# Small loads first, w_up's transpositions ahead of the first mixing, and gates ahead of weight spreading in the first steps of a two-layer kernel

## The chip, the cores and the metric

The kernel runs on one core of a Trainium2 chip. The metric is the device time of one execution in microseconds. The engines are named as in the profile: PE (TensorE), DVE (VectorE), ACT (ScalarE), POOL (GpSimd) and SP (SyncE, which here only issues DMAs). ACT and POOL issue DMAs too; SPq and ACTq are the queues' names.

## The reference

x is 128 batches of 32 channels by 512 columns. Two layers run one after the other, each with a mixing over channels, then a linear layer with a gated low-rank (LoRA) branch, then the residual sum:

```python
# layer 0
h = gelu(cond @ W0 + b0); h = gelu(h @ W1 + b1)          # 128 x 128 each
att = softmax(h @ W2 + b2)                                # 128 x 8, per batch
agg_w = einsum('bk,koi->boi', att, weight); agg_b = att @ bias_k
y = einsum('boi,bih->boh', agg_w, x) + agg_b[:, :, None]
top1 = argmax(y @ gate_w.T + expert_bias)                 # one of 4 experts
x1 = x + y @ W_up.T + (y @ lora_A[top1].T) @ lora_B[top1].T
# layer 1
c = conv1d(x1, weight, 9 taps, 4 groups) + (cond @ c_weight.T)[:, :, None] + fside
p = top2(softmax(c @ W_gate.T)), normalized               # of 8 experts
out = x1 + c @ W_base.T + b_base + sum(p * (c @ A.T) @ B.T)
```

## The kernel before

**Tiles and steps.** The 4096 rows of x are 32 tiles of 128 rows (4 batches). A software pipeline runs 34 steps; in step i TensorE does tile i's first layer (`up_half`, `turn_z`, `lora_delta`), tile i-1's convolution and base product (L1084, L1089), and the mixing `mix(i + 1)` for the next tile. All large products run as three passes over high and low parts of the operands (`up_hi`, `up_lo`, `y_hi`, `y_lo` and so on). Steps 0 to 3 are unrolled, and in steps 0 and 1 the rest of the preparation lies between the tiles' work.

**Order.** Every engine has one block of code and runs it in the order in which it is written; the engines meet in semaphores alone. What is queued behind a wait on an engine waits too.

**The way to the first tile.** The condition is turned (L887), copied (L650), and goes through the MLP: W0 (L890), W1 (L893) with a gelu behind each on ACT, then W2, a softmax, and `att_b`, the attention spread over lanes (L910, L685). The first MLP product waits for W0 and b0 together (`in_mlp[0]`). From `att_b` the mixing weights of a tile come in three steps: `make_prod` on POOL (L401, `prod`), `mix_sums` (L626, two sums `gsum`) and `mix_blocks` (L634, two halves of `mix_w`) on VectorE. Tiles 0 to 4 take their weights this way; from tile 5 they come out of `mix_all`, made at once by `mixb` (L1074, two products of `attT` and `wk_s`) and sent through DRAM. `mix(0, 0)` (L985) multiplies x's tile by these weights; `y_sum` (L644) adds the bias rows (`y`), `y_high` (ACT, L529) and POOL (L475) split it in parts.

**Fills.** All 13 weight operands are transposed by TensorE from the raw loads: `fill(n)` (L881), then `high_part(n)` on ACT (L505; L502 and L503 for `lora_b`), then `low_part(n)` on VectorE (L618, L615). The numbers: 0 to 3 are w_up's column blocks (`up_hi`, `up_lo`; four transpositions of 128x128 each), 4 the gate and `lora_a` rows, 5 (`LB_FILL`) `lora_b`, 6 to 9 `w_base`, 10 `a1` (the next layer's LoRA rows), 11 `bb1`, 12 the second gate. A fill waits for its bank to be free (`bank_free`): 6 for the low part 2, 7 for 3, 8 for 4, 9 for the context bias, 10 to 12 for 6 to 8. The upper halves of w_up's rows are loaded by SP, the lower by ACT (L483).

**Context and taps.** `wctx_s` is turned (L996), copied to `wctxT` (L695) and multiplied by the condition (L1003); `biasT` (L704) comes of it. The convolution's weights are shifted windows of the taps: ACT writes `taps_q` (L539), TensorE turns them in 16 pieces (L1014, into `ps_mix`), and `conv_hi` (L546) and `conv_lo` (L707) are their parts.

**A step.** `up_half(i, 1)` (L921, L926) makes the upper columns and the gate's logits; VectorE adds the bias (`gl`, L809), takes maximum and index, and masks z (`zm`, L825). In steps 0 and 1 `up_half(i, 0)` follows. `turn_z` (L960) transposes the mask, ACT and VectorE split it (`zT`, L516 and L735), `lora_delta` (L968) adds the low-rank product; then x1's two halves (L728), their way through the queues into `xq` (`move_x`, L294: SP five pieces, ACT three), and the next y. Between the instructions of the gate VectorE must wait for its own result, so `mix_sums` of tile i+2 stand there in the first steps (a `memset` of one column, `beat`, otherwise), and `mix_blocks` of tile i+1 ahead of the gate. In front of step 0's gate VectorE waits for `in_rows` (`ebias_s`, `bbase_s`), the last loads of SP's first list.

POOL does, in this order: the copies of `lora_b`, `make_prod(0)` and `(1)`, half of w_base's re-ordering, y_lo(0), the other half, `make_prod(2)`, `order_x(0, 0)` (L407, x's first tile in another order for the residual sum), then the small weights and `make_prod(3)`.

## Time and profile before

| | |
|---|---|
| median of 3 runs | 372.83 us (372.61 to 373.99) |
| the profiled execution | 373.17 us, of it 371.4 in the span |
| mean granted TensorE clock | 0.995 |
| busy share of the span | PE 94%, DVE 64%, POOL 54%, ACT 36% |
| moved by DMA | 31.98 MB, mean 86 GB/s |
| chain that ended last | PE 81%, DVE 4%, DMA 3%, issue 2%, ACT 1% |

The span begins with the first instruction and ends with the last. The profile page gives a mean over preparation and regular tiles; in its 40 slices of 9.3 us PE is at 2, 7, 9, 8 and 8 tenths in the first five, at 9 tenths (that is 90% or more) from the sixth on but for one 6 (the eighth slice, with the wait for `mix_all`), and at 7 and 5 in the last two. Times in the rows below are counted from the span's start.

### The profile page before, as it was taken

To read this page: it belongs to the slowest core of one execution; us is meant where nothing else is said; L and a number is where in the kernel's file an instruction comes from. 1 tells how busy PE (TensorE), PEld (TensorE's weight loads), DVE (VectorE), ACT (ScalarE), POOL (GpSimd) and SP (SyncE) were. 2 spreads that over 40 slices of the span, in tenths; PEclk is the share of its full clock that TensorE was granted. 3 is DMA by queue.
4 is the path that set the end of the run, shared out by engine and by line. 5 is a ranking of instruction groups with operands and counts; after the bars stand their busy time and mean duration, and the time that the engine had idled before them with its cause. 6 is when DMAs were issued, how large, how long until landed. Compare 5 with 4: busy or idle time off the path is not lost.

```text
span 371.4 us, 9133 instructions
## 1 busy us (share of the span) xinstructions
PE 349.1 (94%) x2593; PEld 341.9 (92%) x2593; DVE 238.1 (64%) x977; ACT 135.5 (36%) x410; POOL 199.7 (54%) x229
## 2 busy tenths in 40 slices
PE   2798899699999999999999999999999999999975
PEld 1686789699999999999999999999999999999974
DVE  1677768176666666666766666666667666666653
ACT  1645233134333443323333334333333333343330
POOL 8387546525456665555454565655455545566430
PEclk9999999899999999999999999999999999999999
DMA  7635268523333333333333333444333333332221
GB/s 151 193 103 132 52 170 172 107 46 70 80 77 76 80 85 85 85 85 72 70 57 79 77 76 81 85 85 85 85 64 73 60 80 77 75 83 57 60 58 58
DMA packets 54301, 31.98 MB, mean 86 GB/s; under 512 B 43868, under 2 KB 44300, under 8 KB 54288
## 3 DMA queue, kind: packets, MB, share of 16 engines
q1 hardware_dynamic: 40064, 27.69, 30.8%
q10 hardware_dynamic: 13984, 3.73, 7.2%
q0 software_dynamic: 240, 0.41, 0.4%
q8 instruction: 6, 0.10, 0.1%
q14 instruction: 7, 0.06, 0.0%
HBM read 14.35 MB, written 8.93 MB: 63 GB/s over the span
## 4 chain that ended last, share of the span: by engine, by line
PE 81%; DVE 4%; DMA 3%; issue 2%; ACT 1%; SPq 1%; ACTq 1%; DVEq 0%
PE ps_base L1084 18%; PE ps_up L921 17%; PE ps_base L1089 9%; PE ps_up L926 8%; PE ps_mix L985 7%; PE ps_mix L943 6%; PE ps_conv L943 6%; PE ps_base L1061 6%; PE ps_up L968 3%; DMA xq<-x1s 2%; PE ps_turn L952 1%; PE ps_turn L960 1%; DMA mix_all<-agg_mix 1%; SPq L294 1%; DVE mix_w L634 1%
## 5 line engine op out<-in xcount | busy, mean ns | idle before, releaser
L475 POOL TENSOR_TENSOR y_lo<-y,y_hi 128x512 fp32r<-128x512 f32 x31 | 40.0, 1291 | 123.8 <-ACT y_hi L529 123.8
L1084 PE MATMUL ps_base<-base_hi,c_hi 128*128 128x392 f32 (+1 forms) x256 | 78.2, 322 | 1.8 <-ACT c_hi L576 1.3
L1084 PE MATMUL ps_base<-base_lo,c_hi 128*128 128x392 f32 (+1 forms) x256 | 75.3, 311 | 0.0
L921 PE MATMUL ps_up<-up_hi,y_hi 128*128 128x292 f32 (+1 forms) x256 | 72.0, 304 | 3.1 <-DMA mix_all<-agg_mix 3.1
L921 PE MATMUL ps_up<-up_lo,y_hi 128*128 128x292 f32 (+1 forms) x256 | 69.7, 293 | 0.0
L454 POOL TENSOR_TENSOR xq_lo<-xq,xq_hi 128x260 fp32r<-128x260 f32 x64 | 47.5, 744 | 29.5 <-ACT xq_hi L511 29.5
L463 POOL TENSOR_TENSOR x1b<-x1s,bbase_s 128x256 f32<-128x256 f32 x64 | 56.5, 910 | 0.0
L921 PEld LDWEIGHTS ps_up<-up_hi,y_hi 128*128 128x128 f32 x256 | 49.0, 192 | 4.1 <-issue 4.1
L1084 PEld LDWEIGHTS ps_base<-base_hi,c_hi 128*128 128x128 f32 x256 | 48.2, 188 | 2.3 <-DVE ot L763 2.2
L921 PEld LDWEIGHTS ps_up<-up_lo,y_hi 128*128 128x128 f32 x256 | 49.0, 191 | 0.0
L1089 PE MATMUL ps_base<-base_hi,c_lo 128*128 128x392 f32 (+1 forms) x256 | 48.4, 311 | 0.0
L1084 PEld LDWEIGHTS ps_base<-base_lo,c_hi 128*128 128x128 f32 x256 | 48.1, 188 | 0.0
L511 ACT ACTIVATE xq_hi<-xq 128x260 fp32r<-128x260 f32 x64 | 27.0, 425 | 54.6 <-DMA xq<-x1s 54.6
L529 ACT ACTIVATE y_hi<-y 128x512 fp32r<-128x512 f32 x32 | 20.2, 632 | 69.9 <-DVE y L644 69.9
L926 PE MATMUL ps_up<-up_hi,y_lo 128*128 128x292 f32 (+1 forms) x256 | 43.2, 291 | 0.0
L1089 PEld LDWEIGHTS ps_base<-base_hi,c_lo 128*128 128x128 f32 x256 | 40.7, 189 | 0.0
L407 POOL COPY xtp<-xt 128x512 f32<-128x512 f32 x32 | 38.2, 1194 | 0.0
L926 PEld LDWEIGHTS ps_up<-up_hi,y_lo 128*128 128x128 f32 x256 | 36.9, 190 | 0.0
L576 ACT ACTIVATE c_hi<-ps_ct 128x256 fp32r<-128x256 f32 x64 | 21.1, 382 | 35.2 <-DVE ps_ct L755 35.2
L809 DVE TENSOR_TENSOR gl<-ps_up,ebias_s 128x4 f32<-128x4 f32 x32 | 5.2, 161 | 42.4 <-PE ps_up L926 42.4
L524 ACT ACTIVATE c<-ps_conv,biasT 128x64 f32<-128x64 f32 x128 | 29.7, 315 | 6.3 <-PE ps_conv L943 2.6
L755 DVE STREAM_TRANSPOSE ps_ct<-c 128x256 f32<-128x256 f32 x64 | 29.0, 455 | 1.0
(178 smaller groups left out, 655.0 us busy)
## 6 DMA issues: line engine op xcount, KB each, us to landing
xt<-in_x SPq DMA_DIRECT2D x32, 256.0 KB, 2.7
out_x<-ot SPq DMA_DIRECT2D x32, 256.0 KB, 2.0
xq<-x1s SPq DMA_DIRECT2D x160, 32.5 KB, 2.1
xq<-x1s ACTq DMA_DIRECT2D x96, 32.5 KB, 2.2
rows<-agg_rows SPq DMA_DIRECT2D x2, 597.0 KB, 5.0
wbase_raw<-in_L_ffn_W_base SPq DMA_DIRECT2D x2, 512.0 KB, 4.3
rows<-agg_rows SPq DMA_DIRECT2D x1, 598.0 KB, 4.7
wup_raw<-in_L_ffn_W_up ACTq DMA_DIRECT2D x2, 256.0 KB, 5.0
```

Of the source, the lines that this page charges most:

```text
L407: pool.tensor_copy(xtp[:, par].rearrange("p (j r m) -> p j r m", j=2, r=NQ), columns_of(xt[:, par]))\
L454: pool.tensor_tensor(xq_lo[:, gp], xq[:, gp], xq_hi[:, gp], ALU.subtract)\
L463: pool.tensor_tensor(columns_of(x1b[:, 1 - par])[:, j], shifted(j), columns_of(bbase_s[:])[:, j], ALU.add).then_inc(x1b_done, 1)
L475: pool.tensor_tensor(y_lo[:], y32[:], y_hi[:], ALU.subtract).then_inc(ylo_done, 1)
L511: act.activation(xq_hi[:, gp], xq[:, gp], ACT.Copy).then_inc(xqhi_done, 1)
L524: act.activation(c32[:, 0, cols], ps_of[0][:, 0, cols], ACT.Identity, bias=biasT[:, 0, bass.ds(t * SPT + b, 1)]).then_inc(c32_done, 1)
L755: dve.transpose(ps_ct[:, 0, gp * HALF:(gp + 1) * HALF], c32[:, gp]).then_inc(ct_done, 1)
L921: pe.matmul(into, y_hi[:, k], w[:, k, cols], start=(k == 0 and w is up_hi), stop=False, skip_group_check=True)
L926: mm = pe.matmul(into, y_lo[:, k], up_hi[:, k, cols], start=False, stop=(k == KC - 1), skip_group_check=True)
L943: mm = pe.matmul(ps_of[gp][:, 0, 0:HALF], w[:, gp, part], rhs[:, gp, :, part:part + NB], start=(n == 0 and part == 0), stop=(n == 2 and pa ...
L1084: pe.matmul(ps_base[:, j, 0:width], c_hi[:, q], w[:, q, j, 0:width], start=(q == 0 and w is base_hi), stop=False, skip_group_check=True)
L1089: mm = pe.matmul(ps_base[:, j, 0:width], c_lo[:, q], base_hi[:, q, j, 0:width], start=False, stop=(q == NQ - 1), skip_group_check=True)
```

## The change

Nothing is computed in another way; work changes its place.

- **Loads.** b0 and b1 leave SP's list and are the first two DMAs of ACT. The table load and its dummy activation follow, and ACT's two w_up loads come behind them. On SP `wmix_s` moves from ninth place to fourth.
- **Ahead of tile 0.** TensorE makes fills 0 to 3 in a row ahead of `mix(0, 0)`; the context's turn, its products and fills 4 and 5 stand behind it. ACT makes its high parts 0 to 5 and y_high(0) ahead of `taps_q`. VectorE makes low parts 0 to 2, y(0), low part 3, `wctxT`, low parts 4 and 5. POOL's `order_x(0, 0)` moves ahead of `make_prod(0)`.
- **Taps.** The 16 turns (now `turn_taps`) go from in front of tile 0's up-projection to the end of step 0, behind fill 12; `conv_hi` and `conv_lo` go with them, and TensorE's wait for `conv_lo` from the mixing of tile 1 to the convolution of step 1.
- **Step 0.** `turn_z` no longer waits behind fills 6 to 8: fills 6 and 7 stand between it and `lora_delta(0)`, and 8 to 12 behind `mix(1)`. ACT makes y_high(1) and its three moves right behind high parts 6 and 7; high parts 8 to 12 come behind them.
- **Gates 0 and 1.** VectorE's `mix_blocks(1)` and `(2)` go behind the mask `zm` of steps 0 and 1, and `mix_sums(2)` and `(3)` from between the gate's instructions to behind the next tile's y; `beat` memsets take their places.

The diff, cut to its core:

```diff
--- before.py
+++ after.py
@@ -308,13 +308,11 @@
             sp.dma_start(cond_s[:], cond).then_inc(in_cond, 16)
             sp.dma_start(W0_s[:], W0).then_inc(in_mlp[0], 16)
-            sp.dma_start(b0_s[:], b0.rearrange("(p a) -> p a", a=1)).then_inc(in_mlp[0], 16)
             sp.dma_start(W1_s[:], W1).then_inc(in_mlp[1], 16)
-            sp.dma_start(b1_s[:], b1.rearrange("(p a) -> p a", a=1)).then_inc(in_mlp[1], 16)
+            sp.dma_start(wmix_s[:], wmix.rearrange("k o i a -> o k (i a)")).then_inc(in_mix, 16)
             sp.dma_start(W2_s[:], W2).then_inc(in_mlp[2], 16)
             sp.dma_start(b2_s[:], b2.partition_broadcast(P)).then_inc(in_mlp[2], 16)
             sp.dma_start(biask_s[:], bias_k).then_inc(in_bias, 16)
-            sp.dma_start(wmix_s[:], wmix.rearrange("k o i a -> o k (i a)")).then_inc(in_mix, 16)
@@ -411,6 +409,8 @@
             cp.then_inc(lb_copied, 1)
+            pool.wait_ge(x_in[0], 16)
+            order_x(0, 0)
             pool.wait_ge(attb_ready, 1)
             pool.wait_ge(wmix_ready, 1)
             make_prod(0)
@@ -436,8 +436,6 @@
             make_prod(2)
-            pool.wait_ge(x_in[0], 16)
-            order_x(0, 0)
@@ -478,12 +476,14 @@
+            act.dma_start(b0_s[:], b0.rearrange("(p a) -> p a", a=1)).then_inc(in_mlp[0], 16)
+            act.dma_start(b1_s[:], b1.rearrange("(p a) -> p a", a=1)).then_inc(in_mlp[1], 16)
+            act.wait_ge(ident_ready, 1)
+            act.activation(h1T[:, 0:1], ident[:, 0:1], ACT.Gelu).then_inc(table_loaded, 1)
             for half in range(2):
                 q2 = slice(half * NQ // 2, (half + 1) * NQ // 2)
                 act.dma_start(wup_raw[NB:P, q2], w_up.rearrange("(m j q) h -> j m q h", j=2, q=NQ)[1, :, q2])\
                     .then_inc(in_up[half], 16)
-            act.wait_ge(ident_ready, 1)
-            act.activation(h1T[:, 0:1], ident[:, 0:1], ACT.Gelu).then_inc(table_loaded, 1)
             act.wait_ge(in_mlp[0], 32)
@@ -531,6 +531,10 @@
             act.activation(ex[:], lg[:], ACT.Exp, bias=negm[:, 0:1], accum_out=exsum[:, 0:1]).then_inc(exp_done, 1)
+            for n in range(LB_FILL):
+                high_part(n)
+            y_high(0)
+            high_part(LB_FILL)
@@ -538,12 +542,6 @@
-            for n in range(LB_FILL):
-                high_part(n)
-            y_high(0)
-            high_part(LB_FILL)
-            act.wait_ge(conv_turned, 1)
-            act.activation(conv_columns(conv_hi), conv_turns(), ACT.Copy).then_inc(convhi_ready, 1)
@@ -558,16 +556,13 @@
-                if isinstance(i, int) and i == 0:
-                    high_part(NF1)
-                    high_part(NF1 + 1)
                 if once(i - 1):
                     conv_out(i - 1)
                 if once(i):
                     z_high(i)
                 if isinstance(i, int) and i == 0:
-                    for n in range(NF1 + 2, NF2):
-                        high_part(n)
+                    high_part(NF1)
+                    high_part(NF1 + 1)
                     y_high(1)
@@ -583,8 +578,10 @@
                 if isinstance(i, int) and i == 0:
-                    for n in range(NF2, NF):
+                    for n in range(NF1 + 2, NF):
                         high_part(n)
+                    act.wait_ge(conv_turned, 1)
+                    act.activation(conv_columns(conv_hi), conv_turns(), ACT.Copy).then_inc(convhi_ready, 1)
@@ -688,24 +685,20 @@
-            low_part(0)
-            low_part(1)
-
+            for n in range(NQ - 1):
+                low_part(n)
+            dve.wait_ge(rows_in[0], 16)
+            y_sum(0)
+            low_part(NQ - 1)
             dve.wait_ge(wctx_turned, 1)
             dve.tensor_copy(wctxT[:], ps_conv[:, 0, 0:C].rearrange("p (g o) -> p g o", g=GP).unsqueeze(2)
                             .to_broadcast([P, GP, NP, CG])).then_inc(wctx_copied, 1)
-            low_part(2)
-            dve.wait_ge(rows_in[0], 16)
-            y_sum(0)
-            for n in range(3, NF1):
-                low_part(n)
+            low_part(NQ)
+            low_part(LB_FILL)
             dve.wait_ge(ctx_done, 1)
...
-            dve.wait_ge(convhi_ready, 1)
-            dve.tensor_tensor(conv_columns(conv_lo), conv_turns(), conv_columns(conv_hi), ALU.subtract)\
-                .then_inc(conv_ready, 1)
             mix_sums(1, 0)
@@ -800,22 +793,19 @@
-                elif soon(i + 1):
-                    mix_blocks(i + 1, 0)
-                    mix_blocks(i + 1, 1)
                 if once(i):
...
                     dve.wait_ge(gate0_step, i * G0 + 1)
-                    if soon(i + 2):
+                    if soon(i + 2) and once(i - 2):
                         mix_sums(i + 2, 0)
...
-                    if soon(i + 2):
+                    if soon(i + 2) and once(i - 2):
                         mix_sums(i + 2, 1)
@@ -828,8 +818,9 @@
-                if isinstance(i, int) and i == 0:
-                    low_part(NF1)
+                if isinstance(i, int) and i < 2:
+                    mix_blocks(i + 1, 0)
+                    mix_blocks(i + 1, 1)
@@ -838,7 +829,7 @@
                 if isinstance(i, int) and i == 0:
-                    low_part(NF1 + 1)
+                    low_part(NF1)
@@ -853,9 +844,15 @@
                 if once(i + 1):
                     y_sum(i + 1)
+                if isinstance(i, int) and i < 2:
+                    mix_sums(i + 2, 0)
+                    mix_sums(i + 2, 1)
                 if isinstance(i, int) and i == 0:
-                    for n in range(NF1 + 2, NF):
+                    for n in range(NF1 + 1, NF):
                         low_part(n)
+                    dve.wait_ge(convhi_ready, 1)
+                    dve.tensor_tensor(conv_columns(conv_lo), conv_turns(), conv_columns(conv_hi), ALU.subtract)\
+                        .then_inc(conv_ready, 1)
                     dve.wait_ge(mixb_done, 2)
@@ -977,8 +974,6 @@
-                if isinstance(t, int) and t == 1:
-                    pe.wait_ge(conv_ready, 1)
@@ -989,32 +984,33 @@
-            fill(0)
-            fill(1)
+            for n in range(NQ):
+                fill(n)
+            pe.wait_ge(aggb_ready, 1)
+            mix(0, 0)
             pe.wait_ge(in_ctx, 16)
             pe.wait_ge(attb_ready, 1)
             pe.transpose(ps_conv[:, 0, 0:C], wctx_s[:], ident[0:C, 0:C]).then_inc(wctx_turned, 1)
-            fill(2)
-            pe.wait_ge(aggb_ready, 1)
-            mix(0, 0)
-
+            fill(NQ)
             pe.wait_ge(wctx_copied, 1)
             for gp in range(GP):
                 mm = pe.matmul(ps_conv[:, 0, gp * B:(gp + 1) * B], wctxT[:, gp].rearrange("c p o -> c (p o)"), condT[:],
                                start=True, stop=True)
             mm.then_inc(ctx_done, 1)
-            for n in range(3, NF1):
-                fill(n)
-
-            pe.wait_ge(taps_ready, 1 + GP)
-            pe.wait_ge(y32_done, 1)
-            for part in range(2):
-                for p in range(NP):
-                    s = part * NP + p
-                    mm = pe.transpose(ps_mix[:, 0, s * C:(s + 1) * C],
-                                      taps_q[:, part * NP + NP - 1 - p].rearrange("o g i q -> o (g i q)"),
-                                      ident[0:C, 0:C])
-            mm.then_inc(conv_turned, 1)
+            fill(LB_FILL)
+
+            def turn_taps():
+
...
+                pe.wait_ge(taps_ready, 1 + GP)
+                pe.wait_ge(y32_done, 2)
+                for part in range(2):
...
+                mm.then_inc(conv_turned, 1)
@@ -1027,10 +1023,9 @@
                 if isinstance(i, int) and i == 0:
-                    for n in range(NF1, NF2 - 1):
-                        fill(n)
                     pe.wait_ge(fill_lo, NF1)
                 if isinstance(i, int) and i == 1:
+                    pe.wait_ge(conv_ready, 1)
                     pe.wait_ge(consts_ready, 3)
@@ -1049,7 +1044,8 @@
                     if isinstance(i, int) and i == 0:
-                        fill(NF2 - 1)
+                        fill(NF1)
+                        fill(NF1 + 1)
                     lora_delta(i)
@@ -1065,8 +1061,9 @@
-                    for n in range(NF2, NF):
+                    for n in range(NF1 + 2, NF):
                         fill(n)
+                    turn_taps()
...
```

On TensorE, from w_up's transpositions to tile 0's first up-projection (L921, after L918). Names: `wup_raw` is w_up, `ga_raw` fill 4, `lb_rep` fill 5; 128x128 and the like are the output's shape. Before:

```order
L881 MATMUL ps_up<-ident,wup_raw 128x128 x8
L996 MATMUL ps_conv<-ident,wctx_s 128x32
L881 MATMUL ps_base<-ident,wup_raw 128x128 x4
L985 MATMUL ps_mix<-mix_w,xt 128x128 x4
L1003 MATMUL ps_conv<-condT,wctxT 128x128 x2
L881 MATMUL ps_base<-ident,wup_raw 128x128 x4
L881 MATMUL ps_ct<-ident,ga_raw 128x36 x4
L881 MATMUL ps_turn<-ident,lb_rep 96x128 x4
L1014 MATMUL ps_mix<-ident,taps_q 128x32 x16
L921 MATMUL ps_up<-up_hi,y_hi 128x292
```

After:

```order
L878 MATMUL ps_up<-ident,wup_raw 128x128 x8
L878 MATMUL ps_base<-ident,wup_raw 128x128 x8
L980 MATMUL ps_mix<-mix_w,xt 128x128 x4
L993 MATMUL ps_conv<-ident,wctx_s 128x32
L878 MATMUL ps_ct<-ident,ga_raw 128x36 x4
L997 MATMUL ps_conv<-condT,wctxT 128x128 x2
L878 MATMUL ps_turn<-ident,lb_rep 96x128 x4
L918 MATMUL ps_up<-up_hi,y_hi 128x292
```

All of w_up's sixteen transpositions now stand ahead of the mixing, the context behind it, and the taps are gone from this stretch.

On VectorE, around gate 0, from the context's bias `biasT` to the low part of z (`zT`). Before:

```order
L704 TENSOR_TENSOR biasT<-ps_conv,fside_s 128x256
L707 TENSOR_TENSOR conv_lo<-ps_mix,conv_hi 128x16x2x16
L626 TENSOR_REDUCE gsum<-prod 128x16 x2
L634 TENSOR_TENSOR mix_w<-gsum,quad 128x64 x2
L809 TENSOR_TENSOR gl<-ps_up,ebias_s 128x4
L626 TENSOR_REDUCE gsum<-prod 128x16
L816 MAX m<-gl 128x8
L626 TENSOR_REDUCE gsum<-prod 128x16
L822 MAX_INDEX ix<-m,gl 128x8
L825 SCALAR_TENSOR_TENSOR zm<-iota_e,ix,ps_up 128x96
L618 TENSOR_TENSOR base_lo<-ps_base,base_hi 128x2x256
L735 TENSOR_TENSOR zT<-ps_turn,zT 32x128
```

After:

```order
L700 TENSOR_TENSOR biasT<-ps_conv,fside_s 128x256
L623 TENSOR_REDUCE gsum<-prod 128x16 x2
L799 TENSOR_TENSOR gl<-ps_up,ebias_s 128x4
L805 MEMSET beat 128x1
L806 MAX m<-gl 128x8
L811 MEMSET beat 128x1
L812 MAX_INDEX ix<-m,gl 128x8
L815 SCALAR_TENSOR_TENSOR zm<-iota_e,ix,ps_up 128x96
L631 TENSOR_TENSOR mix_w<-gsum,quad 128x64 x2
L728 TENSOR_TENSOR zT<-ps_turn,zT 32x128
```

The taps' low part and the two halves of tile 1's weights leave the place ahead of the gate; the weights now stand between the mask and z's low part.

On ScalarE, from z's high part in step 0 to the last plane of the preparation (`base_hi` and `b_hi` are the high parts of fills 6 to 12). Before:

```order
L546 ACTIVATE conv_hi<-ps_mix 128x16x2x16
L505 ACTIVATE base_hi<-ps_base 128x2x256 x2
L516 ACTIVATE zT<-ps_turn 96x128
L505 ACTIVATE base_hi<-ps_ct 128x2x256
L505 ACTIVATE base_hi<-ps_conv 128x2x256
L529 ACTIVATE y_hi<-y 128x512
L294 DMA xq<-x1s 128x1x65 x3
L505 ACTIVATE base_hi<-ps_base 128x4x128
L505 ACTIVATE b_hi<-ps_base 128x4x128
L505 ACTIVATE base_hi<-ps_ct 128x4x8
L589 ACTIVATE mix_b<-ps_conv 128x16x32
```

After:

```order
L543 ACTIVATE taps_q<-taps,parity_of 32x16x64 x2
L516 ACTIVATE zT<-ps_turn 96x128
L505 ACTIVATE base_hi<-ps_base 128x2x256 x2
L529 ACTIVATE y_hi<-y 128x512
L294 DMA xq<-x1s 128x1x65 x3
L505 ACTIVATE base_hi<-ps_ct 128x2x256
L505 ACTIVATE base_hi<-ps_conv 128x2x256
L505 ACTIVATE base_hi<-ps_base 128x4x128
L505 ACTIVATE b_hi<-ps_base 128x4x128
L505 ACTIVATE base_hi<-ps_ct 128x4x8
L584 ACTIVATE conv_hi<-ps_mix 128x16x2x16
L586 ACTIVATE mix_b<-ps_conv 128x16x32
```

Two planes of w_base (from `ps_ct` and `ps_conv`) have moved from ahead of tile 1's y_hi to behind the three moves, and `conv_hi` to the end.

## Rows read from the trace of the kernel before

**Rows 1.** The stretches (start:end, length, busy us of PE, PEld, DVE, ACT, POOL, clock, DMA, GB/s).
```profile
2.50:7.10 4.60, 0.45 (x1) 0.18 (x1) 0.55 (x4) 0.98 (x2) 4.60 (x8) 1.00 0.94 177
...
70.57:74.00 3.43, 3.43 (x14) 3.43 (x15) 0.13 (x1) 0.00 (x0) 1.19 (x2) 0.51 0.10 35
...
90.70:360.00 269.30, 268.35 (x2047) 267.87 (x2046) 176.32 (x764) 99.11 (x318) 146.04 (x158) 1.00 0.35 76
```

**Rows 2.** Timeline: start, duration, engine, line, work, count, idle time before and its releaser.
```profile
0.75 1.21 ACTq L483 DMA_DIRECT2D wup_raw<-in_L_ffn_W_up  x2
...
3.26 0.29 DVE L650 COPY condT<-ps_mix 128x128 f32<-128x128 f32 x1 [0.50 <-PE ps_mix L887]
...
7.11 0.80 PE L890 MATMUL ps_mix<-condT,W_s 128*128 128x128 f32 x2 [3.89 <-DMA b_s<-in_L_cond_b]
```

**Rows 3.** The DMA issues: count, KB each, us from issue to landing.
```profile
cond_s<-in_cond SPq DMA_DIRECT2D x1, 64.0 KB, 1.9
...
b_s<-in_L_cond_b SPq DMA_DIRECT2D x2, 0.5 KB, 5.4
```

**Rows 4.** Timeline of TensorE, 14 to 23 us.
```profile
14.64 1.92 PE L881 MATMUL ps_up<-ident,wup_raw 128*128 128x128 f32 x8
...
17.71 1.89 PE L985 MATMUL ps_mix<-mix_w,xt 128*128 128x128 f32 x8
...
19.44 0.61 PE L1003 MATMUL ps_conv<-condT,wctxT 128*128 128x128 f32 x4
...
21.35 1.17 PE L1014 MATMUL ps_mix<-ident,taps_q 32*128 32x32 f32 x16
...
22.46 0.40 PE L921 MATMUL ps_up<-up_hi,y_hi 128*128 128x292 f32 x1
```

**Rows 5.** Timeline of VectorE, 25 to 31 us.
```profile
25.15 1.40 DVE L634 TENSOR_TENSOR mix_w<-gsum,quad 128x64 f32<-128x64 f32 x2
...
26.47 0.15 DVE L809 TENSOR_TENSOR gl<-ps_up,ebias_s 128x4 f32<-128x4 f32 x1
...
27.55 0.31 DVE L825 SCALAR_TENSOR_TENSOR zm<-iota_e,ix,ps_up 128x96 f32<-128x96 f32 x1
...
28.63 0.28 DVE L735 TENSOR_TENSOR zT<-ps_turn,zT 32x128 fp32r<-32x128 f32 x1 [0.17 <-ACT zT L516]
...
30.41 0.69 DVE L644 TENSOR_TENSOR y<-ps_mix,rows 128x512 f32<-128x512 f32 x1
```

**Rows 6.** Timeline of TensorE, ScalarE and ScalarE's DMA queue, 31 to 41 us.
```profile
31.14 2.06 ACTq L294 DMA_DIRECT2D xq<-x1s  x3
...
32.44 1.09 PE L1074 MATMUL ps_conv<-wk_s,attT 8*128 8x512 f32 x2 [0.22 <-DVE base_lo L618]
...
33.24 0.60 ACT L505 ACTIVATE base_hi<-ps_base 128x512 fp32r<-128x512 f32 x1 [1.48 <-issue]
...
34.32 0.40 PE L921 MATMUL ps_up<-up_hi,y_hi 128*128 128x292 f32 x1
...
39.89 0.31 PE L960 MATMUL ps_turn<-ident,zm 128*96 128x128 f32 x1 [0.80 <-DVE zm L825]
...
40.90 0.50 PE L968 MATMUL ps_up<-lb_w,zT 96*128 96x256 f32 x2 [0.70 <-DVE zT L735]
```

**Rows 7.** Timeline of GpSimd, first product; then xt's loads issued before 40 us.
```profile
15.40 0.72 POOL L401 TENSOR_TENSOR prod<-wmix_t,att_b 128x256 f32<-128x256 f32 x1 [5.78 <-DVE att_b L685]
...
DMA to landing us min/median/max: 2.5/4.3/4.6
```

**Rows 8.** The line of mix_w (count, min/median/max ns, us); its longest half in the timeline.
```profile
L634 DVE TENSOR_TENSOR mix_w<-gsum,quad x10: 224/714/1344, 16.7 to 57.4; 128x64 f32<-128x64 f32 x10
...
55.90 1.29 POOL L475 TENSOR_TENSOR y_lo<-y,y_hi 128x512 fp32r<-128x512 f32 x1 [3.63 <-ACT y_hi L529]
...
55.93 1.34 DVE L634 TENSOR_TENSOR mix_w<-gsum,quad 128x64 f32<-128x64 f32 x1 [1.03 <-PE ps_base L1089]
```

**Rows 9.** Timeline of TensorE behind its wait for `mix_all`.
```profile
70.57 0.58 PE L921 MATMUL ps_up<-up_hi,y_hi 128*128 128x292 f32 x1 [3.13 <-DMA mix_all<-agg_mix]
```

5 lines of the change are left out of this document (added).

## The prediction

> **What bounds the kernel now.** I read the stretches first. From 90.70 to 360.00 TensorE is busy 268.35 of 269.30 us [rows 1]: the regular tiles leave nothing to win, and no edit touches them. What can change is how early they are reached, so the sum is made over the way to tile 1's LoRA product (`lora_delta(1)`, at 40.90), behind which both kernels run nearly the same instructions. Next the loads: the first matmul of the conditioning MLP starts at 7.11, after 3.89 us of waiting for a bias [rows 2] whose load takes 5.4 us, while cond_s, issued ahead of it, takes 1.9 [rows 3]; the DMA engines are 94% busy from 2.50 to 7.10 [rows 1]. Then, in order of time, TensorE up to its first up-projection [rows 4], VectorE between there and y(1), the mixed input of tile 1 [rows 5], and the way from y(1) to lora(1) [rows 6].
>
> **A. The small loads.** b0 and b1 go to ACT's queue and are issued first; ACT's two w_up loads (1.21 us of issuing [rows 2]) go behind the table load and its dummy activation. The transposed condition is copied by 3.55 (3.26 + 0.29 [rows 2]), so the first matmul could start at 3.6 where it starts at 7.11, if b0 and W0 have landed. Price of b0: between 1.9, as for cond_s (0.75 + 1.9 = 2.65, hidden under 3.6), and 5.4 as now (0.75 + 5.4 = 6.15). I take the low end: what was ahead of the biases in the engines were ACT's 512 KB, and these are now issued after them. ACT's two issues end near 4.5 (from 3.3, where the dummy activation starts now, plus 1.21), just when the first gelu wants ACT (3.6 + 0.80 + 0.1). wmix, moved from ninth to fourth on SP, is wanted some two us later than it lands. So the chain up to the spread attention comes **3.5 us earlier**. It cannot gain more, since the condition's own load and copy are not moved.
>
> **B. Fills ahead of the first mixing.** TensorE reaches w_up's fills at 11.1 in place of 14.64 [rows 4] and now makes all sixteen transpositions in a row. Eight took 1.92, so sixteen take 3.84 and end at 15.0. The mixing weights are ready at 14.2 (the mixing started at 17.71, less 3.5), so the mixing starts at 15.0, 2.7 earlier; 0.8 of A is lost here. Its eight passes took 1.89, at the slow rate of the transpositions (0.24 us each; the four passes at 19.44 take 0.15 each [rows 4]). The dense block may bring the fast rate sooner: between 0.95 and 1.89, I take 1.5. Its end then lies 3.1 earlier, at 16.5. From there y(0), 0.69 [rows 5], a low plane of equal width, 0.69, the copy of wctxT, 0.4, the context products, 0.6, and lora_b's four transpositions, 0.5 at the fast rate, give 19.4 for the first up-projection, which started at 22.46 [rows 4]: **3.1 earlier**. The sixteen transpositions of the taps (1.17 [rows 4]) no longer stand ahead of it; they come back in D.
> On POOL the copy of x's first tile (`order_x(0, 0)`) now stands ahead of the first product, and the mixing weights behind that. The product started at 15.40 [rows 7] and is wanted at 11.9; a POOL pass this wide takes up to 1.29 [rows 8], so the copy is covered if the tile lands by 10.6. SP issued it at 6.20 and now does so about 1.0 earlier, with two issues fewer ahead; such loads took 4.3 in the median and 4.6 at most [rows 7]: 9.5 to 9.8. Covered, by one us.
>
> **C. Gate 0 ahead of the mixing weights.** Before gate 0 (`gl`, 26.47) VectorE made conv_lo (as wide as y, 0.69) and tile 1's weights `mix_w` (1.40 [rows 5]); both leave, 2.1. Against that, lora_b's planes begin only with the fill that now stands right ahead of the up-projection, where 1.17 of taps lay between; between 0.5 and 1.17 comes back, I take 0.8, because ACT's y_hi(0) is now ahead of these planes instead of among them. So gl is 3.1 + 2.1 - 0.8 = 4.4 earlier. The gate, 1.39 from gl to the end of the mask `zm` (27.86), loses two sums and gets two memsets: between 0.8 and 1.39, I take 1.1, so zm comes 4.7 earlier. Now mix_w(1) sits between zm and z's low part, where 0.77 of waiting and one plane stood (27.86 to 28.63 [rows 5]); at 1.40 that is 0.6 back. **z's low part, and 2.5 behind it as now the end of y(1) (31.10), come 4.1 earlier**, y(1) at 27.0.
> mix_w's price is the uncertain one here. Its ten halves took 0.224 to 1.344, 0.714 in the median [rows 8], so two lie between 0.45 and 2.7. The longest starts 0.03 us after a POOL subtraction of 1.29 and ends 0.08 behind it [rows 8]. I keep 1.40, since POOL copies rows there then as now.
> The Trainium skill ("SBUF — State Buffer", section "SBUF: two separate sides") says that a VectorE instruction with two SBUF inputs and a GpSimd one that reads SBUF lock each other out: the later one waits for the whole earlier one. The row of that longest half agrees. By that rule a half would cost 0.22 when POOL is idle, and the edit would win 0.95 more than I count.
> A wait moves too: gl(0) is now the first behind `in_rows`, the last loads of SP's list. They come about 3.4 earlier by the order of issue; I cost it at nothing, and if they are late by more than the one us of slack, gl and all behind it wait for them.
>
> **D. Taps and spare planes behind tile 1's mixing.** So far ACT made base's third and fourth high planes before y(1). Now they stand behind y_hi(1) and ACT's three xq moves, which end 2.10 after y(1) (31.14 + 2.06 - 31.10 [rows 6]). Then come one high plane, 0.60 [rows 6], its low plane, 0.69, and TensorE's gate fill, 0.5 (y(1) to 32.44 is 1.34 now, less the low plane and 0.15 of waiting for the next one); then the taps, 1.17; then the two mix products, 1.88 (32.44 to 34.32 [rows 6]). So tile 1's up-projection starts 2.10 + 0.60 + 0.69 + 0.50 + 1.17 + 1.88 = 6.9 behind y(1), where it starts 3.2 behind it: **3.7 given back**, and 0.4 of the 4.1 is left. The cover is gone because ACT, not TensorE, now sets this stretch; queued behind its moves are five planes, conv_hi and mix_b.
>
> **E. Gate 1.** mix_w(2) leaves the place ahead of gate 1. TensorE's wait at z's transposition (0.80, for zm) goes, since zm is now ready under the convolution; the wait at lora(1) (0.70, for z's low part [rows 6]) stays about as long, with conv's sum and one transposition ahead of it on VectorE. **0.85 won**, between 0.5 and 1.5 (both waits). For tile 2 the weight sums move behind y(2), POOL's next product waits for them, and y_lo(2) is queued behind that; TensorE waits for tile 1's xq moves right behind y_lo(2)'s use, so I cost it at nothing; without that cover it is some tenths.
>
> **Sum.** 4.1 - 3.7 + 0.85 = 1.25, say 1.3 us. On the profiled execution (373.17, of it 371.4 span) that is 371.9; the median of the runs, 372.83, lies 0.34 below it: **371.5**. Ends: A between 1.0 and 3.5, B half a us either way, mix_w between 0.95 better and 1.3 worse, D between 3.2 and 4.2.
>
> **Rivals.** *The dense block pays more.* Sixteen transpositions without a gap bring TensorE to the fast rate before the mixing (0.95, 0.5 better than my 1.5), and mix_w(1) meets POOL between two copies (0.5 better). For it: both rates and both lengths occur in this trace; against it: POOL's copies stand in the same order. 371.5 - 1.0 = 370.5.
> *The biases land no earlier* (the end on the other side). Place: the first W0 matmul, which waits for b0. Its load is 0.5 KB and took 5.4 us [rows 3]; if that is its own time and not the queue's, the chain starts at 6.15, 2.55 later than my 3.6: 374.0. It decides at 3.6 + 1.3 = 4.9: a landing beyond that makes the kernel slower than before. Against it: the biases stood behind the w_up loads, at engines 94% busy.
> *Clock.* D leaves TensorE little to do for some 4 us before tile 1's up-projection, with one gap near 1.8. Behind the gap of 3.13 in front of 70.57 [rows 9] the granted clock is 0.51 until 74.00, that is the level of 1.2 GHz [rows 1]. If this comes up here, half the clock over 3.43 us loses 1.7: 373.2. Against it: that gap is nearly twice as long. The Trainium skill ("TensorE: Matmul & The Clock Gate", section "HAM oscillation — how this bites in real kernels") warns of idle gaps that re-throttle TensorE; the gap of 3.13 agrees, and no row here shows what a shorter one does.
> *x late.* The upper half of w_up is issued over 2 us later and shares the engines with x's first tile. If that lands at 12.3, not by 10.6, POOL's first product is held 1.7: 373.2. Against it: the latest such load took 4.6, not 7.
>
> **How the numbers follow.** Forecast 0.55, dense block 0.22, biases 0.07, clock 0.08, x late 0.08. The likeliest gives 371.5, by itself 370.8 to 372.4. The range 370.2 to 373.4 takes in all but the biases' 374.0 and the tails. A measurement of this kernel can tell about 0.5% from no change, 1.86 us: below 370.97 lie nearly all of the dense block and the forecast's low edge, 0.26; above 374.69 only late biases with something added, 0.03; between them 0.71.
>
> **What would show it.** Right: the first W0 matmul near 3.6, the mixing near 15, y(1) ending near 27, tile 1's up-projection still near 34 and behind ACT's moves, lora(1) near 39.6. Wrong: a W0 matmul beyond 4.9; a product on POOL that waits for x; a granted clock near half between 28 and 38; a tile 1 up-projection well before 33, which would mean that ACT's moves don't hold the planes.

## The result and the profile after

The change made the kernel slower: 378.17 us in the median against 372.72 of before (four executions of each). The ratio on record is 1.0114 with a 95% interval of 1.0064 to 1.0163; that of these two medians is 1.0146. Forecast were 371.5 and a range of 370.2 to 373.4, so both the time and the sign were missed. The profiled execution took 378.09 us, of it 376.2 in the span: 4.8 over the 371.4 of before.

The page of the changed kernel (the busy tenths and the granted clock in 40 slices, here of 9.4 us) already shows where. Before, the only slice under full clock near the start was the eighth, behind the wait for `mix_all`. Now the fourth and fifth slices, 28 to 47 us, are at 8 and 7 tenths too:

```profile
span 376.2 us, 9139 instructions
...
PE   2877899699999999999999999999999999999985
...
PEclk9998799989999999999999999999999999999999
```

The way through it on TensorE, from the timeline (start, duration, engine, line, work, idle time before and its releaser):

```profile
3.99 0.77 PE L887 MATMUL ps_mix<-condT,W_s 128*128 128x128 f32 x2 [0.47 <-DVE condT L647]
...
9.47 0.60 PE L893 MATMUL ps_mix<-W_s,h2T 128*128 128x8 f32 x2 [3.34 <-DMA b_s<-in_L_cond_b]
...
17.47 1.46 PE L980 MATMUL ps_mix<-mix_w,xt 128*128 128x128 f32 x8
...
21.61 0.38 PE L918 MATMUL ps_up<-up_hi,y_hi 128*128 128x292 f32 x1
...
32.90 0.38 PE L878 MATMUL ps_ct<-ident,g_p 8*128 8x8 f32 x4 [1.91 <-DVE base_lo L615]
...
35.07 1.61 PE L1071 MATMUL ps_turn<-wk_s,attT 8*128 8x512 f32 x2
36.61 0.61 PE L918 MATMUL ps_up<-up_hi,y_hi 128*128 128x292 f32 x1
...
42.24 0.40 PE L940 MATMUL ps_conv<-xq_hi,conv_hi 128*128 128x256 f32 x2
...
45.04 0.50 PE L965 MATMUL ps_up<-lb_w,zT 96*128 96x256 f32 x2 [1.09 <-DVE zT L728]
...
75.23 0.37 PE L918 MATMUL ps_up<-up_hi,y_hi 128*128 128x292 f32 x1 [3.73 <-DMA mix_all<-agg_mix]
```

Against [rows 2, 4, 5, 6, 9] and the sum on record, in us:

| | before | forecast | after |
|---|---|---|---|
| first MLP product | 7.11 | 3.6 | 3.99 |
| first mixing starts | 17.71 | 15.0 | 17.47 |
| tile 0's up-projection | 22.46 | 19.4 | 21.61 |
| mask zm(0) ready | 27.86 | 23.2 | 25.57 |
| y(1) ends | 31.10 | 27.0 | 29.23 |
| tile 1's up-projection | 34.32 | 33.9 | 36.61 |
| tile 1's LoRA product | 40.90 | 39.6 | 45.04 |
| end of the wait for mix_all | 70.57 | | 75.23 |

Two things stand out. The first product came 3.1 earlier, near the forecast's 3.5, but the first mixing only 0.24: the gain was gone within 6 us, in a wait for another bias. And between y(1) and lora(1) 6 us were lost, part of them at half clock. The stretches of the changed kernel (columns as in [rows 1]):

```profile
30.00:35.00 5.00, 2.73 (x26) 2.14 (x27) 3.08 (x5) 3.19 (x6) 2.70 (x3) 1.00 0.73 176
36.00:42.00 6.00, 6.00 (x24) 5.39 (x24) 2.31 (x11) 0.82 (x3) 3.08 (x4) 0.50 0.00 0
```

and the same two of the kernel before:

```profile
30.00:35.00 5.00, 4.18 (x25) 2.67 (x24) 3.03 (x6) 2.39 (x5) 3.42 (x4) 1.00 0.48 68
36.00:42.00 6.00, 4.50 (x36) 4.10 (x35) 5.72 (x18) 2.19 (x9) 4.93 (x6) 1.00 0.27 92
```

From 30 to 35 TensorE had 2.73 us of work in place of 4.18; from 36 to 42 it was busy throughout, with 24 records in place of 36, at 0.50, the level of 1.2 GHz.

One thing is needed to read the runs below. The mean granted clock differs from one execution of a kernel to the next, and the time follows it: before took 371.4 to 373.3 at 0.994 or 0.995, and 375.4 to 376.8 at 0.979 to 0.983. So each kernel is given by its mean clock too, as median us (number of executions). Three executions that are on record as slow (377.07 and 377.94 of before, 375.98 of the mended loads in the old order) count in the first column alone. The columns are coarse, some hold one or two executions, and differences within one are rough:

| kernel | median | 0.993 and over | 0.988 to 0.991 | 0.985 to 0.986 | up to 0.983 |
|---|---|---|---|---|---|
| before, three sets measured beside the runs | 373.3 | 372.3 (31) | 373.8 (20) | 374.3 (6) | 375.9 (7) |
| changed | 378.2 | | | 377.4 (2) | 378.6 (2) |
| changed, last gap filled | 376.6 | | 375.3 (4) | 375.8 (1) | 377.9 (5) |
| changed, planes first | 374.6 | 373.3 (1) | 373.9 (2) | 374.6 (4) | 377.0 (3) |
| changed, loads mended | 377.5 | | | | 377.5 (10) |
| changed, both mended | 373.7 | | | 373.1 (6) | 375.1 (6) |
| changed, all gaps filled | 380.7 | | 376.7 (1) | | 381.9 (3) |
| before, loads alone | 373.5 | 371.6 (2) | 373.2 (5) | 376.4 (1) | 376.5 (2) |
| before, loads mended | 372.5 | 369.6 (2) | 372.0 (4) | 373.4 (2) | 372.7 (3) |
| before, planes late | 376.8 | | 375.9 (3) | 377.5 (2) | |
| before, mix_all early | 368.3 | 368.2 (4) | 369.7 (2) | | |
| before, loads mended, mix_all early | 366.0 | 365.6 (4) | 369.3 (2) | | |

### The profile page after: what moved, and what is told of

Its sections match the earlier page's. It is cut to its first block, busy times and chain, and to the rows that moved or that the text cites. A ratio compares the mean times of both kernels' runs of the same rounds, so it can differ in the third digit from the quotient of the medians.

```text
span 376.2 us, 9139 instructions
## 1 busy us (share of the span) xinstructions
PE 351.5 (93%) x2593; PEld 344.5 (92%) x2593; DVE 240.2 (64%) x981; ACT 135.9 (36%) x410; POOL 200.2 (53%) x229
## 4 chain that ended last, share of the span: by engine, by line
PE 86%; DMA 4%; DVE 4%; issue 2%; SPq 2%; ACT 1%; ACTq 1%; DVEq 0%
PE ps_base L1081 18%; PE ps_up L918 17%; PE ps_base L1086 9%; PE ps_up L923 9%; PE ps_mix L980 7%; PE ps_mix L940 6%; PE ps_conv L940 6%; PE ps_base L1057 6%; PE ps_up L965 3%; DMA xq<-x1s 2%; DMA b_s<-in_L_cond_b 2%; PE ps_turn L949 1%; DMA mix_all<-agg_mix 1%; PE ps_turn L957 1%; SPq L294 1%
## 5 line engine op out<-in xcount | busy, mean ns | idle before, releaser
L918 PE MATMUL ps_up<-up_hi,y_hi 128*128 128x292 f32 (+1 forms) x256 | 72.5, 306 | 3.7 <-DMA mix_all<-agg_mix 3.7
L918 PE MATMUL ps_up<-up_lo,y_hi 128*128 128x292 f32 (+1 forms) x256 | 70.3, 295 | 0.0
L918 PEld LDWEIGHTS ps_up<-up_hi,y_hi 128*128 128x128 f32 x256 | 49.6, 194 | 5.3 <-issue 5.3
L918 PEld LDWEIGHTS ps_up<-up_lo,y_hi 128*128 128x128 f32 x256 | 49.7, 194 | 0.0
L529 ACT ACTIVATE y_hi<-y 128x512 fp32r<-128x512 f32 x32 | 20.2, 632 | 70.9 <-DVE y L641 67.4
L923 PE MATMUL ps_up<-up_hi,y_lo 128*128 128x292 f32 (+1 forms) x256 | 44.3, 296 | 0.1
```

The lines of the kernel that those rows point to most:

```text
L918: pe.matmul(into, y_hi[:, k], w[:, k, cols], start=(k == 0 and w is up_hi), stop=False, skip_group_check=True)
L923: mm = pe.matmul(into, y_lo[:, k], up_hi[:, k, cols], start=False, stop=(k == KC - 1), skip_group_check=True)
```

## Experiments on the loads

**The loads alone, in the kernel before.** The edit is the SP, ACT and `wmix_s` part of the diff, nothing else.

> The kernel before, with the order of the loads alone (part A). Theory: the first product starts near 4.0 in place of 7.11, but the W2 product still near 9.5 (for b2), so the first mixing starts 0.3 to 0.6 before 17.71, and as nothing else is moved, the time is 0.2 to 0.7 less than before: 372.0 to 372.5, the clock as before. Rival, the sum on record for part A: the mixing 2.5 to 3.5 earlier and the time with it: 369.3 to 370.3. Second rival: the loads disturb each other (w_up and x land later): 373 or more.

W2's product waited for b2 until 9.06, the first mixing started at 16.72 and lora(1) at 39.77, 1.13 earlier:

```profile
16.72 1.67 PE L985 MATMUL ps_mix<-mix_w,xt 128*128 128x128 f32 x8
...
39.77 0.50 PE L968 MATMUL ps_up<-lb_w,zT 96*128 96x256 f32 x2 [0.70 <-DVE zT L735]
```

On the way to tile 1 the theory holds, with a little more won than expected (1.0 at the mixing, 0.3 to 0.6 expected), and the 3.5 on record for part A are refuted without any other part of the change. In the time it isn't shown. The median is 373.47 against 373.69 (ratio 1.0009, 0.9961 to 1.0058) where 372.0 to 372.5 were expected. At equal clock the differences go both ways: 0.7 and 0.6 faster in the upper two columns (seven executions), 2.1 and 0.6 slower in the lower two (three). One more thing is in this profile: in spite of the 1.13 won the wait for `mix_all` ended at 70.60, where it ended at 70.57 before [rows 9]:

```profile
70.60 0.58 PE L921 MATMUL ps_up<-up_hi,y_hi 128*128 128x292 f32 x1 [4.62 <-DMA mix_all<-agg_mix]
```

**b2 and GpSimd's zeros, in the changed kernel.** VectorE's copy of wmix had gone from 0.68 us to 2.69. These are the rows of the changed kernel, then that of before:

```profile
5.40 3.54 POOL L394 MEMSET mix_all<- 128x4096 f32 x1
...
6.78 2.69 DVE L649 COPY wmix_rep<-wmix_s 32x1024 f32<-32x1024 f32 x1 [2.94 <-DMA wmix_s<-in_L_cond_weight]
```

```profile
9.55 0.68 DVE L652 COPY wmix_rep<-wmix_s 32x1024 f32<-32x1024 f32 x1 [6.00 <-DMA wmix_s<-in_L_cond_weight]
```

The zeros lie at 5.40 to 8.94 in both kernels. Before, wmix landed behind them; loaded earlier, it starts its copy inside them, and the copy ends 0.53 behind their end, at 9.47: as if it had started at 8.8. The softmax's logits stand behind it on VectorE. So two covers lay over each other, b2 (W2 at 9.47) and the zeros (VectorE till 9.6). Three runs take them away singly and together (cuts of the edits, with a remark behind two lines):

```diff
-            sp.dma_start(b2_s[:], b2.partition_broadcast(P)).then_inc(in_mlp[2], 16)
+            act.dma_start(b2_s[:], b2.partition_broadcast(P)).then_inc(in_mlp[2], 16)   # behind b1
...
-            pool.memset(mix_all[:], 0.0).then_inc(mix_zero, 1)
+                if isinstance(i, int) and i == 1:                                       # in the step
+                    pool.memset(mix_all[:], 0.0).then_inc(mix_zero, 1)
```

b2 alone:

> The changed kernel with b2 on ScalarE's queue behind b0 and b1; GpSimd's zeros stay at 5.40. Theory, two covers: the W2 product starts at 6.8 to 7.7 in place of 9.47, but the copy of wmix still takes about 2.7 and ends about 0.5 behind the zeros, near 9.5, and the logits lg come behind it and lane_rep, at 9.6 to 9.8 in place of 10.18; the first mixing 0.3 to 0.6 earlier than 17.47. Rival, b2 alone held the chain: lg near 8.4, the mixing near 15.7.

The zeros alone:

> The changed kernel with GpSimd's zeros for mix_all in step 1; b2 stays sixth on SP's queue. Theory, two covers: the copy of wmix takes 0.7 to 0.8 in place of 2.69, but the W2 product still waits for b2 until 8.6 to 9.5, and lg comes 0.7 behind it; the first mixing within 0.8 of 17.47. Rival, the engines were held by the zeros in another way too (b2's landing): W2 before 8.4 and the mixing before 16.

Both:

> The changed kernel, with b2's load third on ScalarE's queue in place of sixth on SP's, and GpSimd's 3.54 us of zeros for mix_all moved from 5.40 into step 1 (behind x1b). Theory, two covers for one another: the W2 product waits for b2 until 9.47, and the copy of wmix (2.69 us in place of 0.68, ending 0.53 behind GpSimd's zeros) would hold VectorE till 9.61 in any case; without both the W2 product starts at 7.7 (when W2 lands), the logits lg near 8.4 in place of 10.18, the first mixing near 15.7 in place of 17.47, y(1) ends near 27.4 in place of 29.23. The gap and the half clock behind it stay, so the time is 1.5 to 2 less than the changed kernel: 376.2 to 376.7. Rival: the loads of w_up and x, which now land 7.0 to 7.2 after their issue, or the copy of x ahead of the first product (11.81 to 13.05), hold the mixing: at most 0.7 less, 377.5 or more.

Singly, the logits came at 9.63 and 9.70 in place of 10.18: half a microsecond from either, as the two covers say. With b2 alone W2's product started at 7.03 while the copy took 4.13 (5.35 to 9.48); with the zeros alone the copy took 0.68 while W2's product waited for b2 until 8.99:

```profile
6.52 0.68 DVE L650 COPY wmix_rep<-wmix_s 32x1024 f32<-32x1024 f32 x1 [2.64 <-DMA wmix_s<-in_L_cond_weight]
...
8.99 0.60 PE L894 MATMUL ps_mix<-W_s,h2T 128*128 128x8 f32 x2 [2.83 <-DMA b_s<-in_L_cond_b]
```

Together: W2 at 6.79, lg at 7.50, the first mixing at 14.58 (forecast of the record: 15.0):

```profile
14.58 1.13 PE L981 MATMUL ps_mix<-mix_w,xt 128*128 128x128 f32 x8
```

Each of the single runs was executed once, and neither was faster than the changed kernel: 379.70 at 0.982 with b2 alone, 379.04 at 0.979 with the zeros alone. Even the half microsecond was lost again in the single runs, where the mixing started at 17.35 and 17.47. The rows of the run with b2 alone show to whom:

```profile
5.35 4.13 DVE L649 COPY wmix_rep<-wmix_s 32x1024 f32<-32x1024 f32 x1 [1.44 <-DMA wmix_s<-in_L_cond_weight]
...
10.82 1.02 DVE L663 TENSOR_SCALAR att<-ex,exrec 128x8 f32<-128x8 f32 x1
```

```profile
10.71 1.09 POOL L404 COPY xtp<-xt 128x512 f32<-128x512 f32 x1 [0.62 <-DMA xt<-in_x]
```

`order_x(0, 0)`, which the change put ahead of the first product, ran from 10.71 to 11.80, and VectorE's `att`, 0.23 us in the profile of the changed kernel, ended at 11.84. In the run with the zeros alone `att_spread` took 1.33 in place of 0.42 under the same copy.

With both taken away, too, the time didn't follow the mixing: 377.46 in the median (376.2 to 376.7 were expected), all ten executions at 0.974 to 0.982. y(1) ended at 27.35, 1.9 earlier than without the mending, but the clock now fell near 30.9, and the taps, the two mix products and the up-projection ran at half clock: tile 1's up-projection started at 36.82 (36.61 without). The time is about the rival's (377.5 or more), the mechanism isn't: the mixing did come.

**The mended loads in the old order.** The same edits on the kernel before:

> The kernel before, with the order of the loads (part A), b2 on ScalarE's queue behind b0 and b1, and GpSimd's zeros for mix_all moved into step 1. Part A as the sum on record meant it, in the old order. Theory: as with the same loads in the changed order (lg 7.50, first mixing 14.58), the first mixing starts 2.7 to 3.1 before the 17.71 of before, tile 1's LoRA product near 38.2 in place of 40.90, and the time at equal granted clock is 2 to 2.7 less: 369.6 to 370.3 where the mean clock is 0.995 (before: 371.4 to 373.2, 15 of 31 executions). Rival 1, mix_all: with the loads alone lora(1) came 1.13 earlier and the wait for mix_all still ended at 70.60 (70.57 before); if its landing doesn't follow, the time at 0.995 is 371.5 to 372.3. Rival 2, the clock: a shorter way means the same work with TensorE idle at other places; fewer than a third of the executions keep 0.995 and the median is no better than before.

At 0.995 the two executions took 369.56 and 369.70, 2.6 less than before at that clock: the theory, and what part A is worth when nothing else holds the chain (0.9 to 3.2 less in the other columns). The median, 372.47, is 0.85 less (ratio 0.997, 0.9938 to 1.0002, so not clear of no change). Two of the twelve executions kept 0.995, where eight of the 24 of before beside them had 0.994 or 0.995: rival 2 holds in part. Rival 1 fell. The profiled execution is one at 0.985, so no profile shows the way of those two; in it the first mixing started at 14.62, the clock fell twice, and lora(1) came at 42.62.

## Experiments on the planes behind the moves

**Planes first.** High parts 8 and 9 go back ahead of y_high(1) and the three moves, in the changed kernel:

```diff
-                    high_part(NF1)
-                    high_part(NF1 + 1)
+                    for n in range(NF1, NF2):
+                        high_part(n)
                     y_high(1)
...
-                    for n in range(NF1 + 2, NF):
+                    for n in range(NF2, NF):
                         high_part(n)
```

> The changed kernel, with high parts 8 and 9 back ahead of tile 1's y_hi and ScalarE's three moves, as before the change; all else as changed. Theory, the planes behind the moves (part D): fills 10 to 12 and the taps no longer wait for the end of the moves (31.38); the taps start near 31.1 in place of 33.14, tile 1's up-projection near 34.0 in place of 36.61, no gap of TensorE is over 1 us there, the clock stays at 1.00, and lora(1) comes near 40.0 in place of 45.04: 5 us less, 373 us. Rival, the clock has another cause (the order of the step, the lower load of the engine over a longer stretch): the up-projection is 2 to 2.6 earlier but at half clock, lora(1) near 42.5: 375.5 to 376.2. Second rival: tile 1's moves, issued 0.7 later by ScalarE, hold the convolution: lora(1) over 41, 374 or more.

In the changed kernel the first of the two planes starts when ScalarE's moves have been issued. These are its rows, then the taps of this run:

```profile
29.27 2.11 ACTq L294 DMA_DIRECT2D xq<-x1s  x3
...
31.43 0.60 ACT L505 ACTIVATE base_hi<-ps_ct 128x512 fp32r<-128x512 f32 x1 [1.53 <-PE ps_base L878]
```

```profile
32.36 1.15 PE L1009 MATMUL ps_mix<-ident,taps_q 32*128 32x32 f32 x16
```

The median fell from 378.17 to 374.56, and at equal clock by 2.8 (0.985 to 0.986) and 1.6 (up to 0.983). In the profiled execution the taps started 1.97 behind y(1)'s end (30.39 to 32.36) in place of 3.91 (29.23 to 33.14). The time lies between the theory's 373 and the first rival's 375.5: the order was undone as expected, but the clock still fell in all but one execution to under 0.993.

**Planes late, in the kernel before.** The opposite: the two planes go behind the moves, everything else stays.

> The kernel before, with high parts 8 and 9 behind tile 1's y_hi and ScalarE's three moves: part D's ScalarE side alone; the taps stay where they were. Theory (the price on record for D less the taps): the two mix products wait for low part 9, the moves end 2.10 after y(1), then come two high planes and a low one; tile 1's up-projection starts near 36.9 in place of 34.32, 2.6 later, TensorE has a gap of 2 us or more in front of it, and the time at equal clock is 1.8 to 2.6 over before; with lower clocks in most executions the median is 376 to 377.5. Rival: the stretch behind the up-projection (waits of 0.80 and 0.70 before) takes the delay up: less than 1 over before at equal clock, and 0.995 as often as before.

At equal clock it took 2.1 and 3.2 more than before, the median 376.78 against 373.32 (ratio 1.0096, 1.0062 to 1.0130): over half of the whole loss, from the order of two planes and the clock that fell behind it. TensorE's fill of the gate (fill 12) in the kernel before, then rows of this run, ScalarE's queue and ScalarE first, then TensorE:

```profile
31.84 0.38 PE L881 MATMUL ps_ct<-ident,g_p 8*128 8x8 f32 x4 [0.60 <-DVE base_lo L618]
```

```profile
30.74 2.06 ACTq L294 DMA_DIRECT2D xq<-x1s  x3
...
32.84 0.60 ACT L505 ACTIVATE base_hi<-ps_ct 128x512 fp32r<-128x512 f32 x1 [1.48 <-issue]
...
34.31 0.56 PE L879 MATMUL ps_ct<-ident,g_p 8*128 8x8 f32 x4 [3.46 <-DVE base_lo L616]
...
36.74 1.91 PE L1072 MATMUL ps_turn<-wk_s,attT 8*128 8x512 f32 x2
...
38.58 0.61 PE L919 MATMUL ps_up<-up_hi,y_hi 128*128 128x292 f32 x1
```

The planes start when the moves have been issued (32.80), TensorE waits 3.46 for the low part, and at 34.3 the clock has fallen: the second mix product takes 1.91 in place of 1.02 at full clock. The up-projection starts 4.26 later than [rows 6]. Of that 2.47 stand at the gate's fill already (34.31 against 31.84), where 2.6 were expected for the order; the other 1.79 are added behind it, at half clock.

**Both mended.** The changed kernel with the mended loads and the planes first:

> The changed kernel with both parts mended: b2 and GpSimd's zeros as in the other run, and high parts 8 and 9 ahead of tile 1's y_hi and ScalarE's moves. Theory: y(1) ends near 28 (27.35 with the loads mended, plus up to 0.7), tile 1's up-projection starts 4.9 behind it at full clock, near 32.9, lora(1) near 38.9; at 0.995 that is 370 to 370.8, at 0.982 to 0.986 (three or four stretches at half clock) 373 to 375. Rival: with TensorE busy 7.4 to 7.5 of 10 us in 10 to 20 and 20 to 30 (8.7 and 9.1 before), the clock falls early in nearly every execution, as in the run with the loads mended alone (0.974 to 0.982 in all ten), and the median stays over 374.5.

373.68 in the median, ratio 1.002 (0.9994 to 1.0045). At 0.985 to 0.986 it takes 373.1 where before takes 374.3 and the mended loads in the old order 373.4; up to 0.983 it takes 375.1 against their 375.9 and 372.7 (but three of its six had 0.977, lower than any of the other). So the changed order, mended, is no worse than before at equal clock; whether it is as good as the old order with the same loads stays open. None of its twelve executions kept 0.988 or more, where 21 of the 24 of before beside them did. That is the rival's mechanism; its median, over 374.5, didn't come. In its profile the clock fell first near 20.2, after TensorE had been busy 3.14 of 5 us from 15 to 20.

## Experiments on the clock

**The gap in front of fill 12 filled.** Sixteen transpositions of the identity stand in it; the taps overwrite their result.

```diff
+                    pe.wait_ge(y32_done, 2)
+                    for s in range(16):
+                        pe.transpose(ps_mix[:, 0, 0:P], ident[:], ident[:])
                     fill(NF - 1)
```

> The changed kernel, with sixteen transpositions of the identity (their result is overwritten by the taps) between fill 11 and fill 12, where TensorE now waits 1.91 us (30.99 to 32.90). Theory, the clock: the granted clock falls to 0.50 from 35.3 to 42.6 because of that gap; filled, it stays at 1.00, mix_b's second product takes 1.1 in place of 1.61 and tile 1's up-projection (36.61 to the convolution at 42.24, 5.63) about 3.2, as before the change (34.32 to 37.46); lora(1) then comes near 42.2 in place of 45.04 and the time is 2.5 to 3 less than the changed kernel's 378.2: 375.2 to 375.7. Rival, the order alone: lora(1) is late because of what stands ahead of tile 1's up-projection, the clock falls for another reason or the wait behind it takes the gain: 377.7 to 378.5.

376.64: half the expected gain. Five of ten executions had 0.986 or 0.991, the others 0.982. In the profile TensorE was busy 4.84 of the 5 us from 30 to 35, and the clock still fell, at 36.3 and for 3.4 us in place of 6.8 (35.4 to 42.2): tile 1's up-projection took 4.67 (35.59 to 40.26) in place of 5.63. So the gap of 1.91 is not the only cause; that it made things worse rests on the times and on one profile of each kernel.

**All gaps filled.** Six, five and four more transpositions ahead of the context products, `turn_z` of tile 0 and fill 11:

> The changed kernel with 31 transpositions of the identity in TensorE's waits between 19.5 and 33 us (six ahead of the context products, five ahead of turn_z of tile 0, four ahead of fill 11, sixteen ahead of fill 12); their results are overwritten. Theory, the clock follows how busy TensorE was in the stretch before: with only the last gap filled, five of ten executions had a mean clock of 0.991 in place of 0.982 to 0.986; with all four filled, most have 0.991 or more, and the median is near 375 (at 0.991 the run with one gap filled took 374.3 to 376.3). Rival: what TensorE does ahead of 19 us or the random place of the fall decides; the clock stays at 0.982 to 0.986 in half of the executions or more, median 376 to 377.5.

The median, 380.74, is worse than the rival's: three of the four executions ran at 0.973 to 0.982. As a way to a faster kernel this fell. But the profiled execution, the one at 0.991, had full clock from the start to 70 us, and so shows what the changed order does without the clock. Its timeline on TensorE:

```profile
33.02 0.38 PE L878 MATMUL ps_ct<-ident,g_p 8*128 8x8 f32 x4 [0.25 <-DVE base_lo L615]
...
35.19 1.02 PE L1084 MATMUL ps_turn<-wk_s,attT 8*128 8x512 f32 x2
36.13 0.40 PE L918 MATMUL ps_up<-up_hi,y_hi 128*128 128x292 f32 x1
...
39.29 0.40 PE L940 MATMUL ps_conv<-xq_hi,conv_hi 128*128 128x256 f32 x2
...
42.09 0.51 PE L965 MATMUL ps_up<-lb_w,zT 96*128 96x256 f32 x2 [1.09 <-DVE zT L728]
```

The mixing (17.52) and the end of y(1) (29.26) are those of the changed kernel within 0.05. The up-projection starts 6.87 behind y(1) (6.9 on record for part D), takes 3.16 in place of 5.63, and lora(1) comes at 42.09: 1.19 later than before by the order, and 2.95 earlier than in the changed kernel, which is the clock's part in one profile of each. Why this execution still took 376.74: of the 3.5 by which its span is over that of before, 1.2 stand at the end of the wait for `mix_all` (71.80) and 2.3 behind it, and most of these are seen at the other end, in a stretch at half clock while the last tiles run out (length, PE busy, clock, DMA share, GB/s):

```profile
362.00:366.00 4.00, 3.31 (x17) 0.57 0.01 2
```

## Experiments on the wait for mix_all

**All four loads of mix_all in step 2, in the kernel before.**

```diff
-                if isinstance(i, int) and i in (2, 3):
+                if isinstance(i, int) and i == 2:
...
-                    for s in range((i - 2) * SPT // 2, (i - 1) * SPT // 2):
+                    for s in range(SPT):
```

> The kernel before, with all four loads of mix_all issued in step 2 (before: two in step 2, two in step 3); nothing else is changed. In eight of the ten profiles so far the span was the end of TensorE's wait for mix_all plus 300.7 to 301.1, so whatever moves ahead of it counts only as far as that load moves too. Theory: issued near 56.8 to 59.3 the last load lands by 64.5, ahead of 67.4, when TensorE began to wait for it; the wait of 3.13 goes and with it the stretch at half clock behind it (3.43 us at 0.51, 1.7): 4 to 5 less than before, 367.5 to 369. Rival: the loads, 0.5 MB in front of tile 0's store and tile 5's load, hold the moves of the steps 2 and 3, or the clock falls elsewhere instead: less than 2 gained, 371 or more.

368.32 against 372.89, ratio 0.9892 (0.9853 to 0.9932): the theory. TensorE no longer waits there, nor does the clock fall there (columns: length, PE busy, clock, DMA share, GB/s):

```profile
60.00:70.00 10.00, 10.00 (x80) 1.00 0.90 172
70.00:74.00 4.00, 4.00 (x35) 1.00 0.00 0
```

(The count in this expectation was wrong: the span was the end of the wait plus 300.7 to 301.1 in six of the ten profiles. In the other four it lies between 299.2 and 303.1, by how much of the stretches behind the wait ran at half clock.) In this profile the clock fell at another place, from 33.6 to 37.1, and the execution took 368.29; the one with a mean clock of 1.000 took 368.05. So a fall of that length near tile 1 need not cost the whole of its lost half.

**With the mended loads.**

> The kernel before, with the loads' order, b2 and the zeros as in the run of the mended loads (372.5 in the median, 369.6 at 0.995), and all four loads of mix_all in step 2. Theory: the two gains add up: 4 to 5 less than with the mended loads alone, median 367.5 to 368.5 and 365 to 366 in executions without a stretch at half clock. Rival: earlier by 2.6 the first steps wait for mix_b's way through DRAM or fall to half clock; the median is no better than with mix_all's loads alone.

366.04, ratio to before 0.9853 (0.9802 to 0.9903), 365.6 at 0.993 and over. With mix_all early the loads bring 2.3 in the median (368.32 to 366.04), near their 2.6 alone at 0.995: the gains add up, a little better than expected. This version beats both kernels, by 6.9 and 12.1 us.

## Why the prediction was wrong

**A, the loads: the step that failed.** The biases b0 and b1 did land as taken (2.2 to 2.3 us after their issue, 1.9 taken), and the first product started at 3.99. What failed is the sentence "the chain up to the spread attention comes 3.5 us earlier": `att_b` came 0.59 earlier (14.30 against 14.89). Two things that had been ready in time before now came last: b2, which stayed on SP and took 6.3, and the copy of wmix, "wanted some two us later than it lands", which lands inside GpSimd's zeros. The sum went from the first product straight to the attention and asked neither of the third bias nor of the longest GpSimd instruction in that window, 3.54 us, though GpSimd is busy 4.60 of 4.60 in [rows 1]. ACT's w_up loads, too, went out sooner than the sum took them, at 1.75 and not from 3.3 on, so b2, issued at 3.12, still had their 512 KB ahead of it:

```profile
1.75 1.19 ACTq L485 DMA_DIRECT2D wup_raw<-in_L_ffn_W_up  x2
```

Of 2.7 at the mixing 0.24 remained: 2.46 missing, of which 2.23 still stand at y(1). The run with both mended (mixing at 14.58 in place of 17.47) shows that these two covers held it.

The rule of the Trainium skill ("SBUF — State Buffer", section "SBUF: two separate sides") was cited on record for VectorE instructions with two inputs alone. The same section of the Trainium skill names a plain fp32 copy from SBUF to SBUF too, and any GpSimd instruction against it. The trace agrees: the copy of wmix took 0.68 us clear of the zeros, and 2.69 and 4.13 where it met them, ending 0.5 behind them. For mix_w, where the rule was weighed, it came as written: the halves of tile 1 took 1.25 beside a GpSimd copy, and those of tile 2, with GpSimd idle, 0.35 for both:

```profile
25.48 1.25 DVE L631 TENSOR_TENSOR mix_w<-gsum,quad 128x64 f32<-128x64 f32 x2
...
40.85 0.35 DVE L631 TENSOR_TENSOR mix_w<-gsum,quad 128x64 f32<-128x64 f32 x2
```

```profile
25.42 1.23 POOL L425 COPY a_p<-a_raw 128x256 f32<-128x256 f32 x2
```

**B was right** where A left it: the mixing starts 3.4 behind the start of the sixteen transpositions (3.84 taken), the mixing took 1.46 (1.5), and the up-projection followed 2.7 behind the mixing's end (2.9). "x late" was half right: x landed 7.0 after its issue, at 11.8, not by 10.6; that it cost nothing here was luck, A's own lateness, and with b2 alone the copy then held VectorE's `att` by 0.8.

**C was right.** From the up-projection to `gl` 1.0 was won (1.3 taken), the gate took 0.99 from gl to zm (1.1), and zm to z's low part gave 0.43 back (0.6). The loads behind `in_rows` were in time.

**D was right in its order and wrong in what it did to the clock.** 6.9 from y(1) to the up-projection was forecast, 6.87 measured at full clock, 7.38 in the changed kernel, where the second mix product already ran slowly. The late-planes run shows most of that price in the old order, 2.47 at the gate's fill. The step that failed is the weight of the rival *Clock*, which the sum put at nothing: it had a chance of 0.08 and 1.7 us, and against it stood only that the gap was shorter than that of [rows 9]. All four executions had 0.982 to 0.986, and it cost 2.95 in the profile, since it lay on 5.6 us of up-projection and not on the 3.43 of [rows 1].

**E was right.** From the convolution to lora(1) 2.80 in place of 3.44: 0.64 won (0.85).

**The sum, once more with what was measured.** The way to y(1) -1.87; y(1) to the up-projection +4.16; the up-projection +2.49; convolution to lora(1) -0.64; lora(1) to the end of the wait for mix_all +0.52; behind it +0.14: together +4.80, the difference of the spans. By the order alone (the run with all gaps filled) lora(1) would be 1.19 late; by the record's own steps with A's missing 2.23 it would be 1.0 late. So the two failures are of one size, some 2.2 and 3, and by this sum either would have taken the forecast's 1.3.

**What the prediction left out:** that TensorE waits 3.1 us for mix_all at 70 [rows 9] and that what is won ahead of it counts only as far as mix_all comes earlier too. It was no bar here in the end (the mended loads took 2.6 less at 0.995, though no profile shows that way), but it was the larger gain.

**Open.** What makes the clock fall isn't settled. It fell behind gaps (1.91 in the changed kernel, 3.46 with the planes late), and without one over 1.64 in the 25 us before (the run with the last gap filled, at 36.3); filling all of them gave one execution without a fall near tile 1 and three that were worse. TensorE had been busy for less ahead of the fall in the changed kernel than in the same stretches of before: 8.06 of 10 us from 20 to 30 and 2.73 of 5 from 30 to 35, against 9.07 and 4.18. But that doesn't tell the cause. The run with mix_all early keeps the old order there and was busy for the same 9.07 and 4.18, with no wait over 0.7 in the 20 us before, and its clock fell at 33.6 all the same. Its rows, then those of before (length, TensorE busy, clock, DMA share, GB/s):

```profile
20.00:25.00 5.00, 5.00 (x49) 1.00 0.48 142
25.00:30.00 5.00, 4.07 (x33) 1.00 0.16 56
30.00:35.00 5.00, 4.18 (x19) 0.86 0.54 104
```

```profile
20.00:30.00 10.00, 9.07 (x79) 1.00 0.31 100
30.00:35.00 5.00, 4.18 (x25) 1.00 0.48 68
```

From 10 to 20 it was busy for 8.20 where before was for 8.71; whether that decided, these runs don't show.

## What to carry to other kernels

When a wait is taken off a chain, list everything that the chain meets on its next few steps, with the time at which it is ready now, and look above all at what was ready "in time" only because the chain was late: here one bias and one GpSimd memset took back 2.5 of 2.7 us. A queue that issues DMAs is an engine's time like any other: planes put behind three moves (2.1 us together) set the whole stretch. And give the granted clock of the dense stretch that follows a price in the sum: half clock on tile 1's up-projection cost 2.95 here, over twice what the reordering was to gain.

## What the runs showed of the hardware

- A VectorE copy of 32x1024 fp32 takes 0.68 us with GpSimd idle and 2.69 or 4.13 when it meets a GpSimd memset of 3.54 us; it ends 0.5 us behind that memset. Even a 128x8 `att`, 0.23 alone, took 1.02 beside a GpSimd copy.
- The time of the kernel before goes with the mean granted clock of the execution, from a median of 372.3 at 0.993 and over to 375.9 at 0.983 and below, with the same code.
- The granted clock fell near tile 1 in one profile (33.6, the run with mix_all early) and not in another (before) with the same order of instructions there and the same busy time of TensorE, 9.07 of 10 us and 4.18 of 5.
- Filling TensorE's waits with idle work is no sure way to keep the clock: with 31 added transpositions three of four executions had a mean clock (0.973 to 0.982) no higher than that of the kernel without them (0.982 to 0.986).
- Of loads of 0.5 KB, those issued first landed after 2.2 to 2.3 us; a load of 4 KB issued at 3.12 behind them took 6.3.
